# Sums of self attention on four column groups, with their inverse spread over rows by DMA

## The reference, cut to what matters

```python
q = jnp.einsum('bse,hed->bhsd', x, Wq) + bq[None, :, None, :]
k = jnp.einsum('bse,hed->bhsd', x, Wk) + bk[None, :, None, :]
v = jnp.einsum('bse,hed->bhsd', x, Wv) + bv[None, :, None, :]
scores = jnp.einsum('bhsd,bhtd->bhst', q, k) / jnp.sqrt(jnp.float32(DH))
scores = jnp.where(causal[None, None, :, :], scores, -jnp.inf)
attn = jax.nn.softmax(scores, axis=-1)
out = jnp.einsum('bhst,bhtd->bhsd', attn, v)
out = out.transpose(0, 2, 1, 3).reshape(x.shape[0], seq_len, NUM_HEADS * DH)
return out @ Wo + bo
```

## Time and profile before

| | |
|---|---|
| median of 3 runs | 430.09 us (428.91 to 431.21) |
| profiled execution, its own time | 428.27 us |
| its span | 426.5 us |
| PE, PEld busy | 385.7 us (90%), 274.1 us (64%) |
| DVE busy | 307.5 us (72%) |
| ACT busy | 237.6 us (56%) |
| POOL busy | 239.8 us (56%) |
| main loop in steady state | one slot in 8.62 us |
| chain that ended last, by engine | PE 64%, DVE 14%, ACT 7%, DMA 7% |

### The profile page before, as it was taken

The page is one execution under the profiler, slowest core; times in us unless marked ns, Lnnn a source line. Parts: engine busy times, 40 slices in busy tenths (PEclk is TensorE's granted clock), DMA queues, the critical chain, the costliest instruction groups (busy, mean ns, idle before and its releaser), DMA issues.

```text
span 426.5 us, 9900 instructions
## 1 busy us (share of the span) xinstructions
PE 385.7 (90%) x3698; PEld 274.1 (64%) x3698; DVE 307.5 (72%) x924; ACT 237.6 (56%) x352; POOL 239.8 (56%) x338
## 2 busy tenths in 40 slices
PE   3779999999999999999999999799999999998821
PEld 1567666776767776677766767577787776544410
DVE  0646887877887777887788877976535655689897
ACT  2335665556665566665666556464512155788941
POOL 3466876556665565655667556465824430231775
PEclk9989999999999999999999999999999999999985
DMA  8012011000000300000000000000000000000001
GB/s 259 12 6 54 3 15 27 4 8 5 5 1 5 100 2 2 3 4 1 2 3 2 2 2 3 0 2 2 3 1 2 2 0 2 2 2 2 25 26 51
DMA packets 41568, 6.96 MB, mean 16 GB/s; under 512 B 38320, under 2 KB 40240, under 8 KB 41392
## 3 DMA queue, kind: packets, MB, share of 16 engines
q1 hardware_dynamic: 41520, 6.32, 9.3%
HBM read 5.12 MB, written 1.05 MB: 14 GB/s over the span
## 4 chain that ended last, share of the span: by engine, by line
PE 64%; DVE 14%; ACT 7%; DMA 7%; issue 4%; SPq 3%; POOLq 0%; POOL 0%; DVEq 0%; ACTq 0%
PE banks L172 11%; PE banks L146 10%; PE banks L214 8%; PE banks L699 7%; DMA shift<-neg_max 6%; PE banks L152 4%; PE banks L191 4%; DVE unused L352 3%; PE banks L130 3%; PE banks L743 3%; PE banks L165 3%; SPq L523 3%; PE banks L756 3%; ACT q_hi L305 2%; PE banks L163 2%
## 5 line engine op out<-in xcount | busy, mean ns | idle before, releaser
L286 ACT ACTIVATE probs<-banks 128x768 f32<-128x768 f32 (+1 forms) x96 | 84.9, 884 | 114.1 <-PE banks L152 114.1
L352 DVE CUSTOM_DVE_ANT_0 unused<-banks,neg_mask 128x512 bf16<-128x512 f32 (+3 forms) x256 | 112.6, 487 | 38.8 <-PE banks L130 38.8
L451 POOL TENSOR_SCALAR_AFFINE_SELECT probs<-probs 128x256 f32<-128x256 f32 x128 | 51.2, 412 | 112.7 <-ACT probs L286 111.3
L172 PE MATMUL banks<-probs,v_nat 128*64 128x256 f32 (+3 forms) x512 | 74.4, 433 | 0.0
L172 PEld LDWEIGHTS banks<-probs,v_nat 128*64 128x64 f32 x512 | 36.6, 137 | 45.3 <-issue 40.5
L152 PE MATMUL banks<-shift,ones_r 64*128 64x256 f32 (+3 forms) x256 | 42.9, 329 | 6.7 <-DMA shift<-neg_max 6.6
L898 POOL TENSOR_TENSOR rstd<-var_e,halves 128x4 f32<-128x4 f32 (+1 forms) x16 | 14.4, 898 | 60.1 <-DVE var_e L974 59.8
L146 PE MATMUL banks<-q_hi,k_hi 64*128 64x256 f32 (+3 forms) x256 | 43.5, 334 | 1.7 <-ACT probs L286 1.7
L361 DVE SCALAR_TENSOR_TENSOR q_lo<-banks,bias_qk,q_hi 128x512 fp32r<-128x512 f32 x32 | 24.0, 751 | 25.8 <-ACT q_hi L305 25.8
L146 PE MATMUL banks<-q_hi,k_lo 64*128 64x256 f32 (+3 forms) x256 | 41.9, 321 | 0.0
L146 PE MATMUL banks<-q_lo,k_hi 64*128 64x256 f32 (+3 forms) x256 | 41.8, 320 | 0.0
(11 more groups left out here) (125 smaller groups left out, 826.1 us busy)
## 6 DMA issues: line engine op xcount, KB each, us to landing
shift<-neg_max SPq DMA_DIRECT2D x256, 0.5 KB, 2.0
attn_t<-w_qkv SPq DMA_DIRECT2D x1, 1344.0 KB, 7.0
attn_t<-xT SPq DMA_DIRECT2D x4, 256.0 KB, 7.2
x_s<-x_nat SPq DMA_DIRECT2D x1, 1024.0 KB, 5.1
wo_s<-wo SPq DMA_DIRECT2D x1, 512.0 KB, 3.9
out<-y_out SPq DMA_DIRECT2D x2, 256.0 KB, 3.1
out<-y_out SPq DMA_DIRECT2D x4, 128.0 KB, 1.7
neg_mask<-causal SPq DMA_DIRECT2D x1, 256.0 KB, 3.8
```

The costliest lines, as they stand in the source:

```text
L172: last = mm(o_ps[HALF[h], j * T:S], v_nat[:, v // 2 % 2, j, v % 2, HALF[h]], p_of(v, j, h, 0, S - j * T), start=(j == 0), stop=(j == NT - 1))
L286: nc.scalar.activation(probs[:, v % 2, AT[j]:AT[j] + 2 * n].rearrange("p (h s) -> p h s", h=2), st[:, :, 0:n], ACT.Exp, scale=D ** -0.5).t ...
L352: last = V.tensor_tensor_reduce(out=unused[:, h, at:at + n], in0=mx[:, h, at:at + n], in1=neg_mask[:, S - n:S], scale=-1.0, scalar=3.0e38, ...
L451: return nc.gpsimd.affine_select(out=blk, in_=blk, compare_op=ALU.is_ge, fill=0.0, base=0, pattern=pattern + [[1, T]], channel_multiplier=-1)
```

## The change

The ones have 32 columns, and `sums` writes four groups of 32 rows: for each head the first 256 queries on one group and the second 256 on the next, side by side; `su`, the logarithm, its exponential and the inverse have 256 columns. A new step `spread` of ScalarE issues four DMAs for each unit, which copy one row of the inverse (`r_few`, 256 columns) to 64 rows of `r_neg`. `normalise` waits for them, and is moved to the next slot, between the second maxima and the low half of q. The values are projected in the banks of q and k, one unit later than before, both parts back to back at the start of the slot; the waits follow. The order of the second half and its table of banks are new.

```diff
-        ln_sum = sb("ln_sum", [128, S])
-        r_near = sb("r_near", [128, S])
+        ln_sum = sb("ln_sum", [128, S // 2])
+        r_near = sb("r_near", [128, S // 2])
+        r_few = sb("r_few", [128, S // 2])
         r_neg = sb("r_neg", [128, S])
-        ones64 = sb("ones64", [128, D])
+        ones32 = sb("ones32", [128, 32])
...
-        su = banks[:, 7, :]
+        su = banks[:, 7, 0:S // 2]
...
+        def wide(h, half):
+
+            row = h * D + half * 32
+            return (r_neg[HALF[h], half * S // 2:(half + 1) * S // 2],
+                    r_few[row:row + 1, :].unsqueeze(1).broadcast_to([1, D, S // 2]))
...
             def sums(v):
                 pe.wait_ge(added, 4 * v + 4)
-                if has(v + 2):
-                    pe.wait_ge(v_out, v + 3)
-                elif v:
-                    pe.wait_ge(o_out, v)
+                if v:
+                    pe.wait_ge(neg_out, v)
+                rows = lambda h, half: slice(h * D + half * 32, h * D + half * 32 + 32)
                 for h in (0, 1):
-                    mm(su[HALF[h], 0:T], ones64[:, :], p_of(v, 0, h, 0, T), start=True, stop=True)
+                    mm(su[rows(h, 0), 0:T], ones32[:, :], p_of(v, 0, h, 0, T), start=True, stop=True)
+                    mm(su[rows(h, 1), :], ones32[:, :], p_sum[:, v % 2, h, T:3 * T], start=True, stop=True)
                 for h in (0, 1):
-                    last = mm(su[HALF[h], T:S], ones64[:, :], p_sum[:, v % 2, h, :], start=True, stop=True)
+                    last = mm(su[rows(h, 0), T:2 * T], ones32[:, :], p_sum[:, v % 2, h, 0:T], start=True, stop=True)
                 last.then_inc(sum_done, 1)
 
             def weigh(v):
                 pe.wait_ge(masked, 3 * v + 3)
+                pe.wait_ge(v_out, v // 2 * 2 + 2)
+                if v:
+                    pe.wait_ge(o_out, v)
...
                 if part == 0:
-                    if v >= 3:
-                        pe.wait_ge(o_out, v - 2)
+                    if v < LAST:
+                        pe.wait_ge(ql_out, v + 2)
+                        pe.wait_ge(kl_out, v + 2)
+                    else:
+                        pe.wait_ge(v_out, LAST)
...
-                        last = mm(banks[:, 6 + at, 0:4 * D], x[HALF[h], tile:tile + T],
+                        last = mm(aux[at][:, 0:4 * D], x[HALF[h], tile:tile + T],
...
-                    if v:
-                        pe.wait_ge(ql_out, v)
-                        pe.wait_ge(kl_out, v)
+                    if v == 1:
+                        pe.wait_ge(ql_out, 1)
+                        pe.wait_ge(kl_out, 1)
+                    elif v:
+                        pe.wait_ge(v_out, v - 1)
...
             def slot(u):
                 if has(u):
+                    values(u, 0)
+                    values(u, 1)
                     scores(u, 0)
                 if has(u + 1):
                     maxima(u + 1, 0)
                 if has(u + 2):
                     project(u + 2, 0)
                 if u == LAST - 1:
-                    bias()
-                    context_keys()
-                if has(u + 1):
-                    values(u + 1, 0)
+                    values(LAST, 0)
+                    values(LAST, 1)
                 if has(u):
                     scores(u, 1)
...
                 if has(u + 1):
                     maxima(u + 1, 1)
-                if has(u + 1):
-                    values(u + 1, 1)
...
             def slot(u):
+                if has(u - 2):
+                    spread(u - 2)
                 if has(u):
+                    values(u)
                     exponentials(u, 0)
...
+            def spread(v):
+
+                act.wait_ge(neg_out, v + 1)
+                if v:
+                    act.wait_ge(o_out, v)
+                for h, half in ((0, 0), (0, 1), (1, 0), (1, 1)):
+                    nc.scalar.dma_start(*wide(h, half)).then_inc(wide_in[v % 2], 16)
...
                 if has(u + 1):
                     maxima(u + 1, 0)
                     maxima(u + 1, 1)
+                if has(u - 2):
+                    normalise(u - 2)
                 if has(u + 2):
                     low_half(u + 2, 0)
...
                     inverse(u - 1)
-                    normalise(u - 1)
...
                 if v:
-                    dve.wait_ge(o_out, v)
-                V.scalar_tensor_tensor(out=r_neg[:, :], in0=su, scalar=2.0, in1=r_near[:, :],
+                    dve.wait_ge(wide_in[(v - 1) % 2], 64 * ((v - 1) // 2 + 1))
+                V.scalar_tensor_tensor(out=r_few[:, :], in0=su, scalar=2.0, in1=r_near[:, :],
...
-                dve.wait_ge(neg_out, v + 1)
+                dve.wait_ge(wide_in[v % 2], 64 * (v // 2 + 1))
                 dve.wait_ge(o_done, v + 1)
...
-            exponentials(31, 0); reciprocal(30); exponentials(31, 1); t(0); context(); exponentials(31, 2); q(0)
-            reciprocal(31); t(1); r(0); q(1); s(0, 0, 0); s(0, 0, 1); s(0, 1, 0); s(0, 1, 1); t(2); p(0, 0)
+            exponentials(31, 0); spread(29); reciprocal(30); spread(30); exponentials(31, 1); exponentials(31, 2)
+            reciprocal(31); t(0); q(0); spread(31); t(1); context(); r(0); q(1); s(0, 0, 0); s(0, 0, 1); s(0, 1, 0)
...
```

More of the change, by code:

```diff
@@ L83, in self_attention @@
         ln_out, near_out = sem("ln_out"), sem("near_out")
+        wide_in = [sem(f"wide_in{k}") for k in (0, 1)]
         ql_out, kl_out, max_out, err_out, neg_out, o_out = (
@@ L223, in bias @@
                 pe.wait_ge(later_in, LOADS)
-                pe.wait_ge(ql_out, UNITS)
+                pe.wait_ge(v_out, UNITS)
                 for p in range(PAIRS):
@@ L230, in context_keys @@
             def context_keys():
-                pe.wait_ge(kl_out, UNITS)
+                pe.wait_ge(v_out, UNITS)
                 mm(aux[1][:, 0:B * C], wx_s[:, 1, :], ctx_s[:, :, :].rearrange("p b k -> p (b k)"),
@@ L252, in slot @@
                     maxima(u + 1, 1)
-                if has(u + 1):
-                    values(u + 1, 1)
                 if has(u + 2) and u > -2:
                     project(u + 2, 1)
+                if u == LAST - 1:
+                    bias()
+                    context_keys()
                 if has(u):
@@ L289, in slot @@
             def slot(u):
+                if has(u - 2):
+                    spread(u - 2)
                 if has(u):
+                    values(u)
                     exponentials(u, 0)
+                if u == LAST - 1:
+                    values(LAST)
+                if has(u):
                     exponentials(u, 1)
[L293 to L299, removed]
                 if has(u + 2):
@@ L317, in slot, with values @@
                     reciprocal(u - 1)
+            def values(v):
+                act.wait_ge(v_done, 2 * v + 2)
+                if v >= 4:
+                    act.wait_ge(o_done, v // 2 * 2 - 2)
+                nc.scalar.copy(v_nat[:, v // 2 % 2, v % 2 * 2:v % 2 * 2 + 2, :, :].rearrange("p i a d -> p i (a d)"),
+                               banks[:, 4:6, 0:4 * D]).then_inc(v_out, 1)
             def reciprocal(v):
@@ L333, in _ @@
                     split_x(u // PAIRS + 1)
-            steps["scalar"] = exponentials, reciprocal
+            steps["scalar"] = exponentials, reciprocal, spread
         @block.vector
@@ L497, in _ @@
             nc.gpsimd.memset(kept["halves"][:, :], -0.5)
-            nc.gpsimd.memset(ones64[:, :], 1.0)
+            nc.gpsimd.memset(ones32[:, :], 1.0)
             nc.gpsimd.memset(ones_r[:, :].bitcast(f32), 1.0)
@@ L784, in f @@
                 four(dst, lambda i: xq_t[:, i * T:(i + 1) * T], fkq[:, :], done, False, h)
[L787 to L795, removed]
@@ L796, in _ @@
-            z(2, "b"); s(3, 3); f(1); p(3, 0); p(3, 1); o(3, 0); o(3, 1); u(3); x(2, "a"); z(3, "a"); z(3, "b")
-            x(2, "b"); f(2, "a"); f(2, "b"); x(3, "a"); f(3, "a"); x(3, "b"); f(3, "b")
+            sums(30); scores(31, 0); y(0, 0); y(1, 0); y(0, 1); scores(31, 1); y(0, 2); scores(31, 2); y(0, 3)
+            y(2, 0); y(1, 1); sums(31); weigh(30); y(1, 2); t(0); y(1, 3); q(0); y(2, 1); m(0, 0); m(0, 1)
+            weigh(31); m(0, 2); m(0, 3); m(0, 4); y(2, 2); m(0, 5); m(0, 6); m(0, 7); y(2, 3); t(1); context(); r(0)
@@ new lines, in _ @@
+            q(1); y(3, 0); m(1, 0); s(0, 0); m(1, 1); y(3, 1); m(1, 2); s(0, 1); m(1, 3); y(3, 2); m(1, 4); s(0, 2)
+            m(1, 5); y(3, 3); t(2); s(0, 3); m(1, 6); p(0, 0); m(1, 7); p(0, 1); r(1); q(2); o(0, 0); s(1, 0)
+            m(2, 0); o(0, 1); s(1, 1); m(2, 1); m(2, 2); m(2, 3); t(3); u(0); m(2, 4); s(1, 2); m(2, 5); z(0)
+            s(1, 3); m(2, 6); p(1, 0); m(2, 7); q(3); r(2); o(1, 0); p(1, 1); m(3, 0); s(2, 0); m(3, 1); o(1, 1)
+            m(3, 2); m(3, 3); u(1); s(2, 1); m(3, 4); z(1); s(2, 2); p(2, 0); s(2, 3); m(3, 5); o(2, 0); x(0)
@@ L799, in _ @@
+            m(3, 6); m(3, 7); p(2, 1); r(3); o(2, 1); f(0); s(3, 0); u(2); x(1); s(3, 1); z(2, "a"); f(1); z(2, "b")
```

(30 more changed lines are left out.)

23 lines of the change are left out of this document (9 added, 14 removed), and 14 rows, old and new, of the table USES.

## The result

The changed kernel takes 602.77 us (601.82 to 603.5, 4 runs) against 429.98 us before (4 runs): ratio 1.40, 95% interval 1.397 to 1.406. Forecast were 470 us, 442 to 489: the sign was right, the size of the loss wrong by a factor of four (173 us instead of 42).

What follows compares the result with a forecast made beforehand. TensorE's own list was taken to bound the kernel before; a ring through ScalarE's issues would then set 10.06 us slots instead of 8.62, 29 times, 41.8 us on 428.3, giving 470 us, range 442 to 489.

Steps and rivals of the forecast that it cites:

- The bound before: Main loop: TensorE's own list fills the 8.62 us slot; exponentials finish only 0.31 and 0.25 us before TensorE's next scores.
- The drain: Values back to back on TensorE: the second part waits until the first has drained, 0.22 us a slot.
- the stalls: TensorE ahead of the second and third groups of scores, without values between to cover the exponential: 0.19 and 0.26 us.
- The ring over ScalarE: Inverse, four issues, values' copy, exponential, second scores, maxima, VectorE to next inverse: 10.06 us a slot; forecast given 0.80.
- The step that failed: Spread's landing ahead of the normalisation: claimed to cost nothing at some 2 us, counting only from 4 us on.
- this very sign: Sign of a wrong forecast: idle time ahead of the normalisation that a landing ends, making the DMA's way the price.
- The issues: Four DMA issues on ScalarE's queue between inverse and values' copy: 2.2 us a slot, range 1.45 to 2.6.
- The maxima's rows: Rows carried by SyncE, needed 5.4 us after issue at the second scores: spread beside them would not show.
- The second half at 0: Second half, with three more batches issued and a new order of pieces: costed at 0, range -2 to +6 us.
- The clock: TensorE's granted clock, said to stay full despite over 1 us idle a slot: no cost.
- The sums: Sums on four groups on TensorE: 0.46 us instead of 0.92, so 0.46 us less in each of 32 units.
- The two rivals with cheap issues: ScalarE issues under 0.24 us each: TensorE's list decides, 434 us (0.08); or below 0.19, no exponential stalls, 414 to 421 (0.08).

Runs made afterwards that it cites:

- The run without DMAs: Changed kernel with the spread's four DMAs left out, the normalisation taking a constant in place of the inverse: 443.32 us beside 430.61 for the kernel before.
- the filled run: Changed kernel plus 20 products, results unused, in TensorE's idle time ahead of the projection of q and k: 602.64 us against 602.77.

## Why the prediction was wrong, point by point

- **The bound before** and its thin covers: right. Moving the values out from between the scores cost 0.82 us a regular slot (forecast 0.67). The drain took 0.36 of it instead of 0.22, and the 0.46 that are left for the stalls were forecast at 0.45. The drain's price I had read from a projection at the start of the kernel.
- **The ring over ScalarE**: right as a mechanism, and with 32 source rows also in size (10.2 us against 10.06; issues 2.54 against 2.2). In the changed kernel the other ring, over the landing, decides.
- **The step that failed** is "The landing of the spread costs nothing: ... against landings of some 2 us; it would count from 4 us on." I took the landing from DMAs of 0.5 KB that read 128 rows. The new ones move 64 KB each, all read from one row, and four of them queue up. Their last one lands after 7.89 us, and the ring through it, 14.09 us, sets the slot in place of the 10.06 of the forecast. I had named the limit of 4 us and this very sign as what would prove me wrong, and left the range without it.
- **The issues**: 3.69 us against a range of 1.45 to 2.6. They are long because of the same pieces: with 32 rows they fall to 2.54. Which resource the issue waits for was not shown.
- **The maxima's rows**: "64 KB more per DMA beside them does not show, unless it delays them by over 1 us". It does delay them, by 1.8 us in the median of the stretch above and by up to 6, but TensorE hardly waited for them.
- **The second half at 0**, with -2 to +6: it took 25 us more from the last units on. The run without DMAs, with the same new order, took 3.1 us more there than the kernel before, and the one with 32 source rows 6.6, so most of it is the slow spreads.
- **The clock**: forecast to stay. It fell, and the filled run shows that it cost nothing while the landing set the slot.
- **The sums**: 0.57 us instead of 0.46 for the step; 0.30 instead of 0.46 gained a slot. I had divided the columns by the pace of a step of 1024 columns. That the beginning and end of a short run on four groups weigh more is my guess; no run shows it.
- **The two rivals with cheap issues**, 434 and 414 to 421, fall even with no DMAs at all: 443 us. The Trainium skill's 50 ns of a dispatch (DMA: Bandwidth & Descriptors, "Anatomy of one DMA") stand in a section on DMAs issued by GpSimd, and are not the time for which ScalarE is held: that was 0.47 us at least, like SyncE's. The other sentence that I drew on (same page, "Issuing engines are not separate DMA queues") calls the time to initiate a DMA usually small relative to the DMA itself. The trace agrees with that, 0.73 us against a landing of 6.4 in the median, but it says nothing of what four of them do to a ring.

The Trainium skill would have warned of the landing: SBUF — State Buffer, in "Door 1: The DMA port swizzle", says that DMA bandwidth goes by how many of 16 ports the rows reach, and puts the whole at 436 GB/s. One row reaches one port, an estimated 27 GB/s. The four source rows are 0, 32, 64 and 96, which by the page lie on two ports, an estimated 54 GB/s if both work at once. From the first issue at 253.07 to the last landing at 263.18 the 256 KB make 26 GB/s, near the figure of one port. By the page 16 neighbouring rows reach 4 ports and 32 reach 8, and the pieces took 0.35, 0.10 and 0.06 us with 1, 16 and 32 rows: the same order, but less than in proportion. That the port is the reason is not shown: no run read a few rows of one port, which would tell the port from the row.

## What to carry to other kernels

Cost a DMA by what it reads and writes, not by another DMA's landing time: before a row is copied to many rows from one place, ask whether the value does not already stand on several. A median over all DMAs of one kind can hide those that are issued in a bad moment. A step that is moved onto another engine's queue must be drawn as a ring, with the issue and the landing as two separate ways round; the longer one counts, and shortening the other gains nothing. When work is taken from between two dependent steps, what it covered comes back as stalls: here 0.82 us a slot of moves paid for 0.30 of gain, 18 us against 5 in the times.

## What the runs showed of the hardware

- Reading one row 64 times holds a DMA engine for 0.35 us per piece of 1 KB on average, reading 16 rows four times 0.10, reading 32 rows twice 0.06.
- While such pieces are queued, the issue itself grows, from 0.47 to 1.47 us within one batch of four. SyncE's small DMAs issued in that time land late too: 3.8 us in the median of six, up to 8.1 in the run, against 2.0 otherwise.
- An issue takes ScalarE about as long as SyncE: four in a row took 2.54 us without slow pieces, SyncE's 2.40.
- A part of a product on two row halves that has to wait for the drain of the other costs 0.36 us when nothing stands between (0.71 against 0.35).
- TensorE's granted clock was 1.00 from 252.40 to 254.80 us, then the engine stood idle for 2.65 us, and from 257.40 to 260.20 it was 0.50. With the idle time filled, the slot had 1.00.
